# A graph layer and a ternary feed-forward layer on one core: the high copy moves from ScalarE to VectorE, smaller loads, one product with W_self moved forward

## The reference

```
xn   = layernorm(x)
agg  = segment_sum(xn[src], dst);  neigh = agg / max(degree, 1)
h    = xn @ W_self + b_self + neigh @ W_neigh
h    = layernorm(h) * gamma + beta;  h = where(h >= 0, h, alpha * h)
x1   = x + h + xn
y    = layernorm(x1)
gate, up = y @ Qg.T, y @ Qu.T        # Q*: weights rounded to -1, 0, 1 times a scale per 128 inputs
out  = x1 + (silu(gate) * up) @ Qd.T # 512 -> 1408 -> 512
```

## Time and profile before

| | |
|---|---|
| median of three executions | 1532.24 us (1531.26 to 1532.78) |
| the profiled execution, its own time | 1530.48 us |
| its span, first to last instruction | 1528.0 us |
| TensorE busy | 1477.2 us, 97% |
| VectorE busy | 1050.5 us, 69% |
| ScalarE busy | 1175.0 us, 77% |
| GpSimd busy | 941.5 us, 62% |
| mean granted TensorE clock | 0.995 of full speed |

### The profile page before, as it was taken

One profiled execution on the slowest core, in us unless ns is written; L12 is line 12 of the kernel. 1 busy time (PEld: TensorE's weight loads), 2 busy tenths in 40 slices (PEclk: granted clock), 3 DMA queues, 4 the chain that ended last, 5 costly groups with the idle time before them and its releaser, 6 DMA issues.

```text
span 1528.0 us, 21758 instructions
## 1 busy us (share of the span) xinstructions
PE 1477.2 (97%) x6421; PEld 763.3 (50%) x6422; DVE 1050.5 (69%) x2305; ACT 1175.0 (77%) x2248; POOL 941.5 (62%) x936
## 2 busy tenths in 40 slices
PE   7899998998999999999999999999999998999897
PEld 3444444555555555555555555555555554554343
DVE  8999644566767676675675757667577675765876
ACT  5467720014888888889898897979989998998896
POOL 2113237776777777777777777777777777774000
PEclk9999999999999999999999999999999999999999
DMA  8978459999988888898888878888888888885101
GB/s 309 282 262 260 136 178 336 333 301 279 245 241 250 238 266 248 243 269 215 283 229 253 234 239 246 239 252 233 243 223 245 233 257 242 231 245 145 36 14 41
DMA packets 210386, 353.39 MB, mean 231 GB/s; under 512 B 104986, under 2 KB 104986, under 8 KB 210258
## 3 DMA queue, kind: packets, MB, share of 16 engines
q0 software_dynamic: 70560, 231.27, 52.0%
q1 hardware_dynamic: 139708, 120.73, 26.4%
HBM read 295.79 MB, written 39.62 MB: 220 GB/s over the span
## 4 chain that ended last, share of the span: by engine, by line
PE 84%; DMA 5%; DVE 3%; POOL 3%; issue 2%; SPq 1%; ACT 1%; POOLq 0%; DVEq 0%; ACTq 0%
PE f_ps L971 22%; PE f_ps L972 21%; PE f_ps L785 16%; PE agg_ps L867 11%; PE agg_ps L869 11%; POOL rows L737 3%; PE side_ps L912 1%; DMA x1T<-hsx 1%; DMA rows<-node_table,idx 1%; DMA node_table<-hsx 1%; DMA own_rows<-acc 1%; PE agg_ps L781 1%; DVE st6p L1140 1%; DMA xj<-xnt_rows 1%; PE side_ps L781 1%
## 5 line engine op out<-in xcount | busy, mean ns | idle before, releaser
L737 POOL DMA_INDIRECT rows<-node_table,idx x882 | 893.1, 1013 | 302.5 <-issue 266.0
L1065 ACT ACTIVATE f_ps<-f_ps,ratio 128x512 f32<-128x512 f32 (+2 forms) x1303 | 777.0, 674 | 120.4 <-PE f_ps L972 115.5
L971 PE MATMUL f_ps<-x1T,tern 128*128 128x512 f16 (+2 forms) x1144 | 415.5, 367 | 11.8 <-DMA x1T<-hsx 4.9
L972 PE MATMUL f_ps<-x1T,tern 128*128 128x512 f16 (+2 forms) x1144 | 415.3, 367 | 0.0
L867 PE MATMUL agg_ps<-rows,hot 128*128 128x512 f16 x846 | 323.0, 382 | 7.9 <-DMA rows<-node_table,idx 5.5
L869 PE MATMUL agg_ps<-rows,hot 128*128 128x512 f16 x846 | 320.6, 379 | 0.0
L1415 DVE SCALAR_TENSOR_TENSOR acc<-f_ps,scl,acc 128x512 f32<-128x512 f32 (+2 forms) x143 | 102.3, 716 | 176.5 <-PE f_ps L972 116.3
L971 PE MATMUL f_ps<-hT,tern 128*128 128x512 f16 (+2 forms) x572 | 208.5, 367 | 0.4 <-DVE acc L1415 0.2
L972 PE MATMUL f_ps<-hT,tern 128*128 128x512 f16 (+2 forms) x572 | 208.4, 367 | 0.0
L867 PEld LDWEIGHTS agg_ps<-rows,hot 128*128 128x128 f16 x846 | 119.4, 141 | 115.2 <-issue 35.2
L972 PEld LDWEIGHTS f_ps<-x1T,tern 128*128 128x128 f16 x1144 | 112.1, 98 | 124.7 <-issue 1.8
(11 more groups left out here) (174 smaller groups left out, 1698.9 us busy)
## 6 DMA issues: line engine op xcount, KB each, us to landing
rows<-node_table,idx POOLq DMA_INDIRECT x882
hsx<-own_rows SPq DMA_DIRECT2D x49, 256.0 KB
hsx<-in_x SPq DMA_DIRECT2D x48, 256.0 KB
out_nodes<-work SPq DMA_DIRECT2D x48, 256.0 KB, 3.8
node_table<-work SPq DMA_DIRECT2D x30, 256.0 KB, 2.3
xj<-xnt_rows SPq DMA_DIRECT2D x26, 256.0 KB, 4.5
acc<-own_rows SPq DMA_DIRECT2D x23, 256.0 KB, 4.8
own_rows<-acc SPq DMA_DIRECT2D x23, 256.0 KB, 5.8
```

What stands on the lines that cost most here:

```text
L737: pool.indirect_dma_start(out=rows[:, j, :], out_offset=None, in_=table[:, :], in_offset=bass.IndirectOffsetOnAxis(ap=of[:, j:j + 1], axis ...
L971: pe.matmul(to, lhs, parts[0], start=g == 0, stop=False, skip_group_check=True)
L972: pe.matmul(to, lhs, parts[1], start=False, stop=True, skip_group_check=True).then_inc(p_ff, 1)
L1065: act.activation(ps, ps, ACT.Copy, scale=ratio[:, w if up else 2, j:j + 1]).then_inc(a_scaled, 1)
```

## The change

1. The high copy (L1090) leaves ScalarE's list of work and stands in VectorE's, at the same step, with the same waits; the semaphore `a_hi` becomes `v_hi`.
2. In the table stage, blocks of x from 21 on are loaded one at a time, 19 blocks ahead, where six or seven were loaded at once. The gate weights come in three pieces instead of two, the up weights in six instead of two. gamma, beta and alpha are loaded at block 30 instead of 5, the bias at 32 instead of 6, and `W_self` in four parts at blocks 34 to 37 instead of at once at block 8.
3. `HELD_IN` goes from 5, 5, 5, 4, 4 to 6, 5, 4, 4, 4: slot 0 makes one product more, slot 2 one less.

```
-    HELD_IN = [5, 5, 5, 4, 4]
+    HELD_IN = [6, 5, 4, 4, 4]
+    LOAD_AHEAD = 19
-    PIECES = [(0, 0, 16), (0, 16, NG), (1, 0, 24), (1, 24, NG)] + [(2, FT * i, FT * i + FT) for i in range(KT)]
+    PIECES = [(0, 0, 16), (0, 16, 28), (0, 28, NG)] + [(1, lo, min(lo + 8, NG)) for lo in range(0, NG, 8)] + [
+        (2, FT * i, FT * i + FT) for i in range(KT)]
...
             def load_x(g):
-                hi = min(hi, BLOCKS - 1)
-                if lo >= 3 * GROUP:
-                    sp.wait_ge(a_xn, lo - 2 * GROUP)
+            def load_block(b):
+                sp.wait_ge(a_xn, b - 3 * GROUP + 1)
+                sp.dma_start(xb(b), x[b * P:(b + 1) * P, :]).then_inc(ld_x[b // GROUP + 3], 16)
...
-                if i == 0:
-                    load_piece(1)
+                if i in (0, 2):
+                    load_piece(1 + i // 2)
-                if i == 5:
+                if i == 30:
 ...
-                if i == 6:
+                if i == 32:
 ...
-                if i == 8:
-                    sp.dma_start(wself[:, :, :], W_self.rearrange("(k p) n -> p k n", p=P)).then_inc(ld_self, 16)
+                if 34 <= i < 34 + KT:
+                    k = i - 34
+                    sp.dma_start(wself[:, k], W_self[k * P:(k + 1) * P, :]).then_inc(ld_self, 16)
...
-                if i % GROUP == 5 and i // GROUP + 3 < GROUPS:
-                    load_x(i // GROUP + 6)
+                if 3 * GROUP <= i + LOAD_AHEAD < BLOCKS - 1:
+                    load_block(i + LOAD_AHEAD)
```

In ScalarE's `step(s)` the first part goes; in VectorE's it stands with the same conditions, ahead of the low half's subtraction:

```
-                if s in HIGH_AT:
-                    hc, f = HIGH_AT[s]
-                    u, width = ups(hc, f), WIDTH[hc]
-                    act.wait_ge(v_h, u + 1)
-                    if hc:
-                        act.wait_ge(p_ff, last_use_of_hT(hc - 1, f))
-                    else:
-                        act.wait_ge(p_sd, HELD)
-                    act.activation(hT[:, 0, f, 0:width], acc[:, 1, u % 2, 0:width], ACT.Copy).then_inc(a_hi, 1)
+                if s in HIGH_AT:
+                    ...
+                    dve.tensor_copy(hT[:, 0, f, 0:width], acc[:, 1, u % 2, 0:width]).then_inc(v_hi, 1)
```

More of the change, by code:

```diff
@@ L407, in build @@
             sem(n) for n in ("p_used", "p_deg", "p_sd", "p_own", "p_ff", "p_t4"))
-        a_xx, a_neg, a_x1s, a_hi1, a_scaled, a_silu, a_hi, a_dn = (
-            sem(n) for n in ("a_xx", "a_neg", "a_x1s", "a_hi1", "a_scaled", "a_silu", "a_hi", "a_dn"))
-        v_scaled, v_h, v_hlo, v_out, v_dn = (sem(n) for n in ("v_scaled", "v_h", "v_hlo", "v_out", "v_dn"))
+        a_xx, a_neg, a_x1s, a_hi1, a_scaled, a_silu, a_dn = (
+            sem(n) for n in ("a_xx", "a_neg", "a_x1s", "a_hi1", "a_scaled", "a_silu", "a_dn"))
+        v_scaled, v_h, v_hi, v_hlo, v_out, v_dn = (sem(n) for n in ("v_scaled", "v_h", "v_hi", "v_hlo", "v_out", "v_dn"))
         o_ld, o_hot, o_rows, o_used, o_agg, o_hs, o_sum, o_st, o_dl, o_inv = (
@@ L974, in _ @@
             pe.wait_ge(v_scl, 1)
-            pe.wait_ge(ld_self, 16)
+            pe.wait_ge(ld_self, 16 * KT)
             for t in range(SLOTS):
@@ L1300, in _ @@
                 for b in range(done, upto):
-                    if b % GROUP == 0:
-                        dve.wait_ge(ld_x[b // GROUP + 3], 16)
                     if b == BLOCKS - 1:
                         dve.wait_ge(ld_xlast, 16)
+                    elif b >= 3 * GROUP:
+                        dve.wait_ge(ld_x[b // GROUP + 3], 16 * (b % GROUP + 1))
+                    elif b % GROUP == 0:
+                        dve.wait_ge(ld_x[b // GROUP + 3], 16)
                     block_stats(b)
@@ L1411, in step @@
                     dve.wait_ge(a_silu, u + 1)
-                    after(dve, a_hi, u - 1)
+                    after(dve, v_hi, u - 1)
                     after(dve, v_hlo, u - 1)
@@ L1423, in step @@
                     add_own(i)
+                if s in HIGH_AT:
+                    hc, f = HIGH_AT[s]
+                    u, width = ups(hc, f), WIDTH[hc]
+                    dve.wait_ge(v_h, u + 1)
+                    if hc:
+                        dve.wait_ge(p_ff, last_use_of_hT(hc - 1, f))
+                    else:
+                        dve.wait_ge(p_sd, HELD)
+                    dve.tensor_copy(hT[:, 0, f, 0:width], acc[:, 1, u % 2, 0:width]).then_inc(v_hi, 1)
                 if s in LOW_AT:
@@ L1426, in step @@
                     u, width = ups(lc, f), WIDTH[lc]
-                    dve.wait_ge(a_hi, u + 1)
+                    dve.wait_ge(v_hi, u + 1)
                     dve.tensor_tensor(hT[:, 1, f, 0:width], acc[:, 1, u % 2, 0:width], hT[:, 0, f, 0:width],
```

## The result

The changed kernel takes 1537.79 us (median of 17 executions) where the kernel before, beside it on the same chip, takes 1532.18 (17 executions). The ratio is 1.0036, 95% interval 1.0025 to 1.0047: 5.5 us slower, where 5.2 us faster was forecast. The profiled execution took 1537.79 us, with a span of 1535.7 (before 1528.0), so its span is 7.7 us longer.

What follows compares the result with a forecast made beforehand. TensorE was taken to bound the main stage, nearly full GpSimd second, 0.5 us per slot behind. Table stage -3.2, HELD_IN -3.4, copy's gather delay +1.0, tail +0.4 sum to -5.2 us: 1532.24 becomes 1527.0, range 1521 to 1534.

Steps and rivals of the forecast that it cites:

- The table stage's term: Table stage, smaller and later loads: removing TensorE's gap at 56 us gains 3.2 us, bounds 0 and 4.6.
- What is late next: Table stage, blocks 21 to 27: VectorE's group scales let TensorE be earlier by 3.5 us at most, of 6.6.
- I take the gap as gone: Table stage, 56 us: block 4's store lands in 4 to 5 us instead of 9.69, ending TensorE's 4.74 us wait.
- The clock should stay up: Table stage, TensorE: no lower clock follows the remaining wait, since a 3.3 us wait in slot 0 brought none.
- HELD_IN: Slots 0 to 2: slot 0's added product hides in 6.3 us of gather waits, gaining 3.4 us, bounds 0 and 3.4.
- The copy's duration: VectorE: each moved copy runs like a cast, about 0.4 us, with 0.69 as upper bound.
- The copy in front of slot 12: Gathers ahead of slot 11: copies delay GpSimd 0.2 us per slot over six slots, 1.2 us lost.
- The mean gather: GpSimd, profile after: 1.02 to 1.04 us expected; 1.08 or more with row waits in slots 40 to 48 means gathers bound.
- The wait at 1261 us: Main stage, TensorE's 4.93 us wait: fewer ScalarE copies bring it forward by perhaps 1 us, capped by the gathers.
- The tail: After the gathers: twenty copies on VectorE cost 0.4 us, bounds -1 and +3.
- Rival 1: GpSimd's queue, slots 6 to 48: copies make the gathers the bound, 1533.4 us up to about 1550; chance 11%.
- Rival 2: Table stage: the gap at 56 us only moves, block 4's store being issued late by SyncE; 1530.2 us; chance 17%.

## Why the prediction was wrong

The sum was -3.2 - 3.4 + 1.0 + 0.4. It should have read about +2.7 - 2.9 + 4.3 + 1.4, by the runs above. The 2.7 is what copy and HELD_IN leave of the whole, and the 4.3 is the copy's 5.7 us less the 1.4 from slot 37 on, so it is no test that this sum comes out. Measured directly, slots 6 to 13 give +3.5 us.

- **The table stage's term failed**, and the step is "or grow by the 0.8 us that SyncE's two added instructions put ahead of that transpose". VectorE's one wait of 1.12 us became 1.27 + 4.09, and the group's scales came 3.85 us late. The two added instructions are there as counted (0.9 us). But the second transpose was issued 3.9 us later (48.41, before 44.56): the first transpose took SyncE 3.19 us instead of 1.33, and the store of block 3 took 1.28 instead of 0.36. The first transpose also landed 2.0 us later after its issue (9.6, before 7.6). I had counted instructions at 0.4 us each and left out that the same instruction can hold the queue longer; that DMAs in flight do this is likely, and not shown.
- **What is late next** was right, down to the figure: without new waits on VectorE the turns from 22 on gain 3.4 to 3.5 us and no more, as the run with the three DMAs moved shows. **"I take the gap as gone"** held in part. The store of block 4 landed in 4.2 us, as forecast, but was issued 2.0 us later, and block 11 waits for the store of block 3. Turns 13 to 20 gain 3.6 to 3.7 us of the 6.6.
- **"The clock should stay up"** failed too: behind the wait of 3.86 us at block 21 the granted clock was 0.72, and 1.75 us of the 2.2 that turn 22 is late arise there. The turn of 0.99 us instead of 0.60 behind the old gap in the earlier trace rows had shown such a clock. And the lower bound of 0 for the term left no room for a loss.
- **HELD_IN** was right in time: -2.9 measured, -3.4 forecast. Its sign in the profile, waits for rows of 3 us or less, was not met (4.6 and 4.5).
- **The copy's duration** was right (0.42 us). The Trainium skill's tier table ("VectorE: DVE Perf Modes", "The perf-mode tier table") gave 0.42 as an estimate, and the row agrees.
- **The copy in front of slot 12 was mis-sized**, in the step "so 0.07 us per copy, with 11 copies in four slots 0.2 us per slot". Measured are 3 to 5 us more for the 90 gathers of slots 7 to 11 (121.4 to 123.6 us, before 117.9 to 118.9), in which 16 copies stand: 0.2 to 0.3 us per copy. In time this is +3.5 us (1.8 to 5.2) instead of +1.2. The place was right, and the condition also (no margin in slot 11, plenty from 14 on). The price came from a lock of 0.25 us seen from VectorE's side, taken as if it met copies at random. How a copy slows the gathers is not shown: most of those inside a gather leave it alone, and a longer copy costs the gathers no more. The mean gather, which the forecast had as its sign, hides this: over 400 to 1400 us it is 1.020 us, before 1.018.
- **The wait at 1261 us**, which I had coming forward by perhaps 1 us, is still 4.87 us (before 4.93).
- **The tail**: +0.4 forecast, +1.4 measured from slot 37 on, within the bound of 3. Each copy stands between VectorE's rescaling and product steps, where 19.0 of 20 us are busy (1420 to 1440).
- **Rival 1** (11%) had the slower gathers, but with the table stage's gain kept (1533.4) and with 4.1 us more behind slot 38, where none were lost. **Rival 2**, that the gap only moves, came true in part by its own way (the store of block 3 was held up by SyncE's queue) and in part by another, the late scales. No case held both. Rival 1's rule in the Trainium skill ("SBUF — State Buffer", "Who interferes with whom") has the copy block GpSimd for its whole length; 32 of the 50 copies inside a gather go against it. The same section lets operations with two SBUF inputs delay only GpSimd's reads, and infers that descriptor generation isn't held up by them. By that the two-input copy should have kept the gathers' pace; the measured 122.4 us instead of 117.9 to 118.9 go against it.
- **The profile before flattered**: it shows no wait for rows in slots 11 and 12 and a distance of 9.5 us in slot 11, where six others on the quick chip have 7.9. I knew that its own time lay 1.8 us below the median, and used that only to shift the sum.

## What to carry to other kernels

When a stage waits on a DMA, read the issuing queue's own timeline before the loads are rearranged: what holds the queue may be something that could be issued any time (here three DMAs, 6 us, worth -3.7 us), and a smaller transfer that starts earlier may delay a third engine's work. When a wait is removed, price what the released engine's partner will wait for, with its clock step, also on the downward side. Work moved to VectorE can cost where GpSimd's DMAs have no margin: price it by the time that a fixed number of gathers takes with it and without, in several executions, and leave it to ScalarE there. In slots 14 to 36, where a slot's first gather is issued about 13 us or more ahead of its use, it cost nothing. And before a loss is put down to a place, look at how much that place varies without the change.

## What the runs showed of the hardware

An indirect DMA's issue on GpSimd (mostly 0.95 us) took up to 2.13 us in the kernel before and 2.10 in the changed one (2.59 with the two-input copy), beside VectorE work without a pause in the case shown. The 90 gathers of slots 7 to 11 took 3 to 5 us longer with 16 copies on VectorE, and no longer with two-input copies of 0.68 us than with plain ones of 0.42. A gather that had the subtraction `hT<-acc,hT` of 512 elements as VectorE's latest instruction 0.45 us after its start was over 1.0 us long in 13 of 50 cases before and 24 of 51 after; with the product that has one input in PSUM (L1415) it was in 2 of 59. SyncE's issue of one DMA took from 0.26 to 5.0 us on the quick chip: the same padding DMA took 4.48 us at block 4 and 0.43 at block 24. And the same kernel took 1532 us on at least three chips and 1716 to 1721 on two others, at a granted clock of 0.99 and 0.97, by rows that land later.
